# Two mixture-of-experts stages with row tiles of 128 in place of 256

## What is computed

```
# stage "top2": context picks the experts
combine = one_hot(top_k(context @ Wg + bg, 2)) * softmax(of the two)
h = relu(einsum('bsd,edf->bsef', layernorm(x), W1) + b1)      # 256 -> 1024
x = x + einsum('bsed,bse->bsd', einsum('bsef,efd->bsed', h, W2) + b2, combine)
# stage "top1": x picks one expert, each takes C = 4096/8 = 512 rows
h  = relu(einsum('ecm,emh->ech', disp, w1) + b1)
eo = einsum('ech,ehm->ecm', h, w2) + b2
x  = x + eo[slot] * gate_val
```

## Time and profile before

| | |
|---|---|
| median of 3 runs | 1720.63 us (1719.39 to 1721.53) |
| the profiled execution | 1719.23 us |
| its span, first to last instruction | 1717.2 us |
| top2: first PE tile, last matmul, next stage begins | 97.4, 544.3, 565.1 us |
| top1: first PE tile, last matmul, next stage begins | 635.7, 821.1, 846.1 us |
| mean granted TensorE clock | 0.862 of 2.4 GHz |

### The profile page before, as it was taken

The page is one execution under the profiler, slowest core; times in us unless marked ns, Lnnn a source line. Parts: engine busy times, 40 slices in busy tenths (PEclk is TensorE's granted clock), DMA queues, the critical chain, the costliest instruction groups (busy, mean ns, idle before and its releaser), DMA issues. The chain is left out here.

```text
span 1717.2 us, 31944 instructions
## 1 busy us (share of the span) xinstructions
PE 1314.6 (77%) x10558; PEld 1071.9 (62%) x10559; DVE 1208.4 (70%) x2055; ACT 821.3 (48%) x1215; POOL 512.8 (30%) x589
## 2 busy tenths in 40 slices
PE   6179999999996629899139999999999179761077
PEld 3169888888896319788127888878888045320066
DVE  3869765666553569866068788888787877898944
ACT  3447433333332317533025565565565046886764
POOL 0045666666653024564212222233221000000000
PEclk9579999999998759999658888888888579996589
DMA  9457433333322556632410000000000100235311
GB/s 326 149 160 212 99 51 50 50 51 51 50 43 26 182 173 198 168 56 33 109 58 10 10 10 12 9 9 9 9 10 1 55 1 1 111 134 219 123 44 56
DMA packets 103397, 134.31 MB, mean 78 GB/s; under 512 B 16144, under 2 KB 87440, under 8 KB 101520
## 3 DMA queue, kind: packets, MB, share of 16 engines
q1 hardware_dynamic: 81808, 103.33, 18.2%
q0 software_dynamic: 21504, 29.83, 10.6%
HBM read 88.43 MB, written 44.70 MB: 78 GB/s over the span
## 5 line engine op out<-in xcount | busy, mean ns | idle before, releaser
L600 ACT ACTIVATE top_x_all<-top_h_ps,top_b1T 128x256 f32<-128x256 f32 x448 | 186.3, 473 | 316.3 <-PE top_h_ps L480 316.1
L478 PE MATMUL top_h_ps<-top_xT_hi,top_w_hi 128*128 128x256 f16 x896 | 246.5, 275 | 3.0 <-DVE top_xT_lo L779 1.6
L479 PE MATMUL top_h_ps<-top_xT_lo,top_w_hi 128*128 128x256 f16 x896 | 246.5, 275 | 0.0
L480 PE MATMUL top_h_ps<-top_xT_hi,top_w_lo 128*128 128x256 f16 x896 | 246.3, 275 | 0.0
L496 PE MATMUL top_y_ps<-top_w_hi,top_x_all 128*128 x896 | 244.4, 273 | 0.3 <-DVE top_x_all L792 0.3
L497 PE MATMUL top_y_ps<-top_w_lo,top_x_all 128*128 x896 | 244.4, 273 | 0.0
L498 PE MATMUL top_y_ps<-top_w_hi,top_x_all 128*128 x896 | 244.3, 273 | 0.0
L358 POOL DMA_INDIRECT x_sum<-top_x_all,top_rows_out x112 | 186.9, 1669 | 116.4 <-POOL top_rows_out L354 85.0
L790 DVE CAST top_x_all<-top_x_all 128x512 f16<-128x512 f32 x224 | 101.2, 452 | 145.6 <-ACT top_x_all L600 145.5
L792 DVE TENSOR_TENSOR top_x_all<-top_x_all 128x512 f16<-128x512 f32 x224 | 155.4, 694 | 7.7
L346 POOL DMA_INDIRECT top_xg<-normed,top_rows_in x112 | 122.3, 1092 | 90.1 <-POOL top_rows_in L343 88.1
(11 more groups left out here) (293 smaller groups left out, 3121.3 us busy)
## 6 DMA issues: line engine op xcount, KB each, us to landing
top_staged<-in_L_xattn_W SPq DMA_DIRECT2D x32, 512.0 KB, 5.9
top_staged<-in_L_ffn_w SPq DMA_DIRECT2D x32, 512.0 KB, 6.3
up_raw<-ffn_u_all SPq DMA_DIRECT2D x48, 256.0 KB, 2.1
ffn_yT<-up_raw SPq DMA_DIRECT2D x12, 1024.0 KB, 4.8
normed<-top_x_all SPq DMA_DIRECT2D x2, 4096.0 KB, 14.1
top_w_lo<-in_ctx SPq DMA_DIRECT2D x4, 1024.0 KB, 9.7
top_x_all<-in_x SPq DMA_DIRECT2D x4, 1024.0 KB, 11.9
x_sum<-top_x_all SPq DMA_DIRECT2D x4, 1024.0 KB, 11.1
```

The lines of the kernel that those rows point to most:

```text
L478: nc.tensor.matmul(out, hi, xT_hi[p][:, c, :], start=(c == 0), stop=False)
L479: nc.tensor.matmul(out, hi, xT_lo[p][:, c, :], start=False, stop=False)
L480: last = nc.tensor.matmul(out, lo, xT_hi[p][:, c, :], start=False, stop=(c == DC - 1))
L600: last = nc.scalar.activation(h32[:, fc * R:(fc + 1) * R], h_ps[:, b, q * R:(q + 1) * R], ACT.Relu, bias=b1T[:, bass.ds(e * FC + fc, 1)], ...
```

## The change

`R` becomes 128. top2 has 72 tiles (8192 rows and the rounding of eight parts, then rounded to a multiple of eight), top1 32. `AHEAD` becomes 8: eight gather buffers of 128 rows each (the same memory), and loop bodies of eight tiles; gathers run ten tiles ahead in place of six. The head stays eight tiles. Each tile has one gather and one add. Layer 1 keeps its 48 matmuls with 128 moving columns; layer 2 has 24, with 256.

```diff
-    R = 2 * P
+    R = P
+    AHEAD, EARLY = 8, 10
+    PAIRS = AHEAD // 2
     if capacity is None:
         NT = (choices * tokens + E * (R - 1)) // R
-        NT += -NT % 4
+        NT += -NT % AHEAD
...
-    NS = 2 * NT
+    NS = NT
...
-        AHEAD, EARLY = 4, 6
...
-        xg = [sb(f"xg{b}", [P, 2, DW], F32)[:] for b in range(AHEAD)]
+        xg = [sb(f"xg{b}", [P, DW], F32)[:] for b in range(AHEAD)]
...
-        HEAD = 2
+        HEAD = 1
...
+            def add(q, i):
+                m, p = PAIRS * q + i // 2, i % 2
+                free(pool, s_added[1 - p], 16 * (m + p))
...
                 for c in range(DC):
-                    for k in range(2):
-                        last = nc.tensor.transpose(xT_ps[p][:, c * R + k * P:c * R + (k + 1) * P],
-                                                   xg[i][:, k, c * P:(c + 1) * P], ident[:])
+                    last = nc.tensor.transpose(xT_ps[p][:, c * R:(c + 1) * R], xg[i][:, c * P:(c + 1) * P], ident[:])
...
-                for k in range(2):
-                    out = y_ps[p][:, k * D:(k + 1) * D]
-                    rows = slice(k * P, (k + 1) * P)
-                    nc.tensor.matmul(out, h_hi[p][:, fc, rows], hi, start=(fc == 0 and k == 0), stop=False, skip_group_check=True)
-                    nc.tensor.matmul(out, h_hi[p][:, fc, rows], lo, start=False, stop=False, skip_group_check=True)
-                    last = nc.tensor.matmul(out, h_lo[p][:, fc, rows], hi, start=False, stop=(fc == FC - 1), skip_group_check=True)
+                out = y_ps[p][:, 0:D]
+                nc.tensor.matmul(out, h_hi[p][:, fc, :], hi, start=(fc == 0), stop=False, skip_group_check=True)
+                nc.tensor.matmul(out, h_hi[p][:, fc, :], lo, start=False, stop=False, skip_group_check=True)
+                last = nc.tensor.matmul(out, h_lo[p][:, fc, :], hi, start=False, stop=(fc == FC - 1), skip_group_check=True)
...
-                free(dve, s_added[1], 16 * (2 * m + p - 1))
+                free(dve, s_added[p], 16 * m)
```

More of the change, by code:

```diff
@@ L163, in experts @@
         at += 2 * FC * R
-        y = [flat[:, at + p * 2 * D:at + (p + 1) * 2 * D].rearrange("p (k d) -> p k d", k=2) for p in range(2)]
-        AHEAD, EARLY = 4, 6
+        y = [flat[:, at + p * D:at + (p + 1) * D] for p in range(2)]
         xT_hi = [sb(f"xT_hi{p}", [P, DC, R], F16) for p in range(2)]
@@ L227, in experts @@
         expert_of_tile = sb("expert_of_tile", [P, NT], I32)
-        rows_in = [[sb(f"rows_in{p}{k}", [P, 1], I32) for k in range(2)] for p in range(AHEAD)]
+        rows_in = [sb(f"rows_in{b}", [P, 1], I32) for b in range(AHEAD)]
         rows_out = [sb(f"rows_out{p}", [P, 1], I32) for p in range(2)]
@@ L311, in _ @@
                 load_expert(e)
-            for k in range(2):
-                sp.wait_ge(s_added[k], 16 * NT)
+            for p in range(2):
+                sp.wait_ge(s_added[p], 16 * M)
         @block.gpsimd
@@ L335, in _, with gather @@
             nc.gpsimd.memset(ones32[:], 1.0).then_inc(s_const, 1)
-            def gather(q, i, k):
+            def gather(q, i):
                 q, i = q + i // AHEAD, i % AHEAD
[L340 to L344, removed]
+                m, p = PAIRS * q + i // 2, i % 2
+                free(pool, s_wc[p], m - PAIRS + 1)
+                rows = rows_in[i]
+                nc.gpsimd.tensor_copy(rows[:], row_of_slot[:, bass.ds(AHEAD * q + i, 1)]).then_inc(s_rows_in[p], 1)
+                pool.wait_ge(s_rows_in[p], m + 1)
@@ L345, in gather @@
                 pool.sem_inc(s_go)
-                nc.gpsimd.indirect_dma_start(out=xg[i][:, k, :], out_offset=None, in_=normed,
+                nc.gpsimd.indirect_dma_start(out=xg[i], out_offset=None, in_=normed,
                                              in_offset=bass.IndirectOffsetOnAxis(ap=rows[:, 0:1], axis=0)
                                              ).then_inc(s_xg[i], 16)
[L350 to L355, removed]
+            def add(q, i):
+                m, p = PAIRS * q + i // 2, i % 2
+                free(pool, s_added[1 - p], 16 * (m + p))
+                nc.gpsimd.tensor_copy(rows_out[p][:], row_of_slot[:, bass.ds(AHEAD * q + i, 1)]).then_inc(s_rows_out[p], 1)
+                pool.wait_ge(s_rows_out[p], m + 1)
@@ L361, in add_and_gather @@
             def add_and_gather(q):
                 for i in range(AHEAD):
-                    for k in range(2):
-                        add(q, i, k)
-                        gather(q, i + EARLY, k)
+                    add(q, i)
+                    gather(q, i + EARLY)
             pool.wait_ge(s_table, 1)
@@ L370, in _ @@
             for i in range(EARLY):
-                for k in range(2):
-                    gather(0, i, k)
+                gather(0, i)
             if gate_source is not None:
@@ L378, in _ @@
             for j in range(NT - 2 * AHEAD, NT):
[L379 to L382, removed]
+                add(j // AHEAD, j % AHEAD)
+                if j + EARLY < NT:
+                    gather(j // AHEAD, j % AHEAD + EARLY)
         def w1_at(w, e, dc, fc):
@@ L605, in _ @@
             x_high(0, 0)
-            for m in range(2 * HEAD):
+            for m in range(PAIRS * HEAD):
                 for p in range(2):
@@ L611, in _ @@
                     hidden(m, p, 2 * m + p)
[L612 removed]
+            with act.Fori(PAIRS * HEAD, M - 1) as m:
                 for p in range(2):
```

33 lines of the change are left out of this document (14 added, 19 removed).

## The result

The changed kernel takes **1886.53 us** (median of 4 runs, 1883.65 to 1888.97), against 1720.99 in runs of the kernel before beside it: **1.0963** of its time (95% interval 1.0949 to 1.0977), 165.5 us more. Forecast were 1846 us and a range of 1822 to 1890. The direction and the limit behind it came out as forecast. The size is 40 us short, and nearly all of that lies in one place: top2's loop, whose code is loaded again at every jump (31 us in all in the two tiles at each jump, 8 in the other tiles of these rounds).

A forecast was written before the change was run, and what follows sets the result against it. The prediction took the array to bound the kernel before and PE's sequencer the changed one. Its terms, -19.7 - 21.3 + 107.6 + 81.0 - 9.3 - 13.5 = +124.8 us, led to 1846 us, range 1822 to 1890.

The forecast's parts named there:

- The sequencer paces, 7.1 us a tile: Steady tiles: PE's sequencer needs 7.1 us for 128 rows, against 10.9 for 256 before; 81 in 100.
- four register instructions in a free stretch: PE after standing empty at 188 us: L497's register instructions 0.74 us apart, so 0.75 us taken for a block.
- The array needs 5.6 us: Steady tiles: the array needs 5.6 us for 128 rows, with 57 ns for each 128-column matmul.
- Rivals 1 and 2: Steady tiles: the array paces, 1714 us (6 in 100); small matmuls cost more than their columns say (5 in 100).
- rival 3: Steady tiles: PE's clock falls to half; for a quarter of the time +88 us, 1934 us; 8 in 100.
- 2 us to spare: Heads: the array streams 5.6 of 9.5 us, nearer to a clock fall, but with 2 us to spare.
- The head: First eight tiles of a stage: split steps of 9.5 us instead of 11.2; top2 19.7 us earlier, top1 21.3.
- The ends: From a stage's last matmul to the next stage: 11.5 us, so -9.3 us in top2 and -13.5 in top1.
- The loops: Jumps back in the loops: each redoes one look-up, some 1 us; six jumps in top2, one in top1.
- this line of the table: top2 from tile 8 to the last matmul: 463.4 us against 355.8, +107.6 us.
- My allowance of 3 us: Code loading at the loops' jumps: 0 to 3 us each, 0 to 21 in all, taken as 0.

The follow-up runs named there:

- shift27: The changed kernel with 27 more small transposes at the start of top2's program on PE, moving later PE instructions by 54 places: 1849.88 us, 1.0752.
- static_all: The changed kernel with PE taking expert 0's weights at fixed addresses after a stage's first eight tiles, without register instructions for addresses: 1705.95 us, 0.9917.
- static_l2lo: The changed kernel with one of six register instructions in a PE block gone, the one for layer 2's low weights: 1822.10 us, 1.0600.
- more_regs: The kernel before with more address work on PE, 80 register steps for a tile instead of 48, same matmuls: 1779.83 us, 1.0347.
- body4: The changed kernel with a loop body of four tiles, four gather buffers and gathers six tiles ahead; tiles of 128 rows stay: 1862.95 us, 1.0838.

## Why the prediction was right, and where it was 40 us short

- *The sequencer paces, 7.1 us a tile* (81 in 100): right. 520 and 524 matmuls in 50 us; 7.07 us a tile in the last eight of top2, 7.1 in shift27's loop. The forecast rested on four register instructions in a free stretch; static_all, static_l2lo and more_regs show that they are the cause. static_l2lo gives 0.11 to 0.12 us for one of them. If all six of a block cost that, they make up some 0.69 of its 0.75 us, which answers the question that the prediction had to leave open: the three matmuls less save the sequencer next to nothing.
- *The array needs 5.6 us*: 5.52. Rivals 1 and 2 fall with the same run: it is below the sequencer, and a 128-column matmul costs 56 ns.
- *The clock* (rival 3): in the loops it did not fall through the thinner stream of matmuls. It fell for 6.8 us behind each stop of 5.5 us, behind a jump without a reload for 3.4 us or not at all (body4: behind eight of top2's fourteen), and with the stops gone it stood at 1.00 over most of the loop (shift27: from 287 to 635 us). In the heads it did fall, where the prediction had "2 us to spare": in top2 it was 0.50 in four stretches of 3.4 us (the first at 118.5, the last until 169.7), while before it stood at 1.00 from 105.8 to 549.5. What it cost there no run tells apart; DVE's splits set the pace, and tile 8 still began 3.9 us ahead of the forecast.
- *The head*: six splits in 54.5 us (103.90 to 158.44), 9.1 a step where I took 9.5, and 1.5 us earlier at the start; -3.9 us in top2 and -1.5 in top1.
- *The ends*: 13.1 and 13.7 us instead of 11.5. After top2's last matmul an older add was still to be issued (673.66), not half done.
- *The loops*: **this term was mis-sized** (forecast 7 us for jumps and 0 for code). "A jump back redoes one look-up, some 1 us", and for the code "0 to 3 us each, 0 to 21 in all, and take 0". What the jumps of top2 cost is read between the changed kernel and shift27: 31 us in the first two tiles of the six rounds (21.0 in place of 15.8 us), 8 us in their other tiles. That is 39 of the 43.8 us by which this line of the table exceeds the forecast; the rest is six jumps that cost 1.6 without a reload in place of 1.0, and the rounding of 7.1. My allowance of 3 us counted the load alone. It left out the half clock that follows a stop (1.8 us), and the slower tiles of a round that is being loaded. The range had room for 21 us of code loading and not for 39; that 1886.5 still lies inside it, 3.5 us from its end, is in part luck: the heads came 5.4 us shorter than the sum had them, and top1's one jump happened to begin at a place where nothing reloads (in shift27 it did, for 5 us).
- *What I argued with.* "In five rounds of the old loop no packet of q8 came ... so the body stays loaded" was true of 65 KB and says nothing of 103. The Trainium skill (Advanced Engine Details and Errata, section on the ISA cache) gives TensorE 128 KB in 16 KB lines. The packets are 16 KB here, and bodies of 103 KB stayed loaded in some places, one of 130 KB never did. But by size alone the changed kernel's body fits, and it did not stay: the runs show that the place of its ends counts too, and nine packets a round say that lines beyond the body are brought in as well. My "with a line or none to spare" was the right warning, and I gave it no weight in the sum.
- *Gather buffers*: POOL never held PE in the loop; with four buffers (body4) the tiles were the same.

Open stays how lines are replaced: a boundary at 44 or 80 reloads at every jump, at 120 at the first only, at 175 or 246 never. I read these from packet times, which may be off by some 30 instructions. All places but 120 and 121 fit one count, an estimate from these places: a body that touches eight packets reloads and one that touches seven does not. The shorter body of static_l2lo fits too. In top2 it needs eight by a few instructions and reloaded at all six jumps, in top1 (boundary at some 55, counted on from top2's in the order of the program) it needs seven, and its branch took 0.23 us. No run tests this count by itself.

## What to carry to other kernels

A matmul whose address comes from a register costs the sequencer as well as the array; count both for a tile, since halving a tile halves only the array's part. When a change lengthens a loop body, look at the loop's branch and at the instruction queue's packets inside the loop, and price a reload at each jump with what follows it; whether a body of some 100 KB stays loaded is a matter of where it starts, and 54 instructions ahead of it were worth 2% here. Where an index is known in advance, write it in as a number: in top1 that, with the splits spread out, turned the small tile's loss of some 50 us into a gain of 6.

## What the runs showed of the hardware

- On PE's sequencer a register instruction for an address costs 0.11 to 0.12 us (static_l2lo, for the address of layer 2's low weights).
- A float16 matmul of 128 columns with a weight load of its own starts 0.056 us behind the one before it at the full clock (static_all).
- A reload at a loop's jump: 3.3 to 5.2 us in the branch, then mostly 6.8 us at half clock (3.4 to 10.2 in all runs). In the changed kernel it makes 6.8 us in all (21.0 for two tiles of 7.1), against 1.6 without.
- While a loop round is being loaded its tiles are 0.2 us slower (7.33 and 7.10), though packets come 9 us apart.
- The same 103 KB loop ran in 1850 or 1886 us by where it began: 54, 180 or 220 more instructions ahead of it gave 1850, 1856 and 1884.
